# A list scheduler's priorities and assumed durations, changed in an attention and feed-forward layer

## The reference

```python
# step 1: causal attention on the normalised rows, 16 heads of 16 numbers
qkv = layernorm(x) @ w_qkv                       # then Q, K, V per head
Q, K = apply_rope(Q), apply_rope(K)              # rotate by position
attn = softmax(where(causal, Q @ K.T * 0.25, -1e6))
x = x + (attn @ V) @ w_proj + b_proj
# step 2: two products, and the length of the pair
y = layernorm(x)
x = x + sqrt((y @ cos(theta + theta_noise))**2 + (y @ sin(phi + phi_noise))**2)
```

## Time and profile before

| what | value |
|---|---|
| time, median of 3 executions (lowest to highest) | 1993.34 us (1989.42 to 1999.2) |
| the profiled execution: its own time, and its span | 1999.2 us, 1997.5 us |
| PE busy, share of the span | 1951.3 us, 98% |
| DVE | 1562.7 us, 78% |
| ACT | 1390.4 us, 70% |
| PEld (weight loads) | 796.1 us, 40% |
| POOL | 871.5 us, 44% |
| DMA, mean of 16 engines | 67 GB/s, 0.2 of their time |

### The profile page before, as it was taken

One profiled execution on the slowest core, in us unless ns is written; L12 is line 12 of the kernel. 1 busy time (PEld: TensorE's weight loads), 2 busy tenths in 40 slices (PEclk: granted clock), 3 DMA queues, 4 the chain that ended last, 5 costly groups with the idle time before them and its releaser, 6 DMA issues.

```text
span 1997.5 us, 38166 instructions
## 1 busy us (share of the span) xinstructions
PE 1951.3 (98%) x12020; PEld 796.1 (40%) x12020; DVE 1562.7 (78%) x4101; ACT 1390.4 (70%) x2687; POOL 871.5 (44%) x1336
## 2 busy tenths in 40 slices
PE   7999999999999999999999999999999999999998
PEld 4333432344434434344343343434443344333334
DVE  5898799977878788786887878788777758978735
ACT  3456777876676787766777777777767676777774
POOL 4714525445245463464445354453443545231222
PEclk9999999999999999999999999999999999999999
DMA  6301312122121221312222131222212131030131
GB/s 142 95 24 28 120 38 80 39 69 73 38 68 54 84 87 65 93 43 65 61 73 78 44 103 37 97 61 67 79 30 76 58 99 59 27 99 8 47 102 58
DMA packets 130762, 133.30 MB, mean 67 GB/s; under 512 B 29434, under 2 KB 105722, under 8 KB 130554
## 3 DMA queue, kind: packets, MB, share of 16 engines
q1 hardware_dynamic: 127728, 128.29, 21.0%
q10 hardware_dynamic: 2832, 2.56, 0.7%
HBM read 38.49 MB, written 25.68 MB: 32 GB/s over the span
## 4 chain that ended last, share of the span: by engine, by line
PE 85%; ACT 5%; issue 3%; DVE 2%; POOL 2%; DMA 2%; SPq 1%; DVEq 0%; ACTq 0%; POOLq 0%
PE banks L1059 22%; PE banks L1074 22%; PE banks L1037 22%; PE banks L981 6%; PE banks L992 5%; ACT probs L1178 3%; PE banks L926 3%; PE banks L1019 3%; DVE chunk_max L1379 1%; DMA squares<-sums 1%; SPq L739 1%; PE banks L915 1%; PE banks L908 1%; PE banks L1045 0%; ACT L1178 0%
## 5 line engine op out<-in xcount | busy, mean ns | idle before, releaser
L1178 ACT ACTIVATE probs<-banks 128x512 f32<-128x512 f32 (+1 forms) x2240 | 1144.5, 602 | 356.3 <-PE banks L1059 270.1
L1379 DVE TENSOR_REDUCE chunk_max<-banks 128x1 f32<-128x512 f32 x1536 | 987.3, 683 | 246.3 <-PE banks L1037 243.3
L1059 PE MATMUL banks<-stack_q,stack_k 99*128 99x512 bf16 (+3 forms) x2560 | 736.5, 350 | 12.1 <-ACT probs L1178 4.3
L1037 PE MATMUL banks<-stack_k,stack_q 96*128 96x512 bf16 (+3 forms) x2560 | 709.7, 349 | 11.0 <-DVE chunk_max L1379 4.5
L1374 DVE CUSTOM_DVE_ANT_0 banks<-banks,row_mask 128x128 f32<-128x128 f32 (+3 forms) x1024 | 483.9, 508 | 74.1 <-PE banks L1037 72.9
L1074 PE MATMUL banks<-probs,v_one 128*17 128x512 f32 (+3 forms) x5120 | 531.0, 533 | 2.0 <-POOL probs L1506 0.8
L1059 PEld LDWEIGHTS banks<-stack_q,stack_k 99*128 99x128 bf16 x2560 | 230.6, 97 | 430.3 <-ACT probs L1178 229.0
L1037 PEld LDWEIGHTS banks<-stack_k,stack_q 96*128 96x128 bf16 x2560 | 232.9, 97 | 328.9 <-DVE chunk_max L1379 80.9
L1506 POOL TENSOR_SCALAR_AFFINE_SELECT probs<-probs 128x512 f32<-128x512 f32 x256 | 161.9, 641 | 378.4 <-ACT probs L1178 378.0
L1074 PEld LDWEIGHTS banks<-probs,v_one 128*17 128x17 f32 x5120 | 118.0, 96 | 263.7 <-issue 177.8
L1374 DVE DVE_READ_ACCUMULATOR2_ANT chunk_max<- 128x1 f32 x1024 | 144.2, 141 | 0.0
(11 more groups left out here) (158 smaller groups left out, 1162.2 us busy)
## 6 DMA issues: line engine op xcount, KB each, us to landing
stack_q<-parts SPq DMA_DIRECT2D x384, 64.0 KB, 2.6
stack_k<-parts SPq DMA_DIRECT2D x354, 64.0 KB, 2.6
sums<-o_raw SPq DMA_DIRECT2D x64, 256.0 KB, 2.4
rot<-raw SPq DMA_DIRECT2D x236, 64.0 KB, 2.0
xin<-x SPq DMA_DIRECT2D x16, 512.0 KB, 3.9
mid<-x SPq DMA_DIRECT2D x13, 512.0 KB, 4.9
heads_t<-sums SPq DMA_DIRECT2D x26, 256.0 KB
inverse<-inverses SPq DMA_DIRECT2D x26, 256.0 KB
```

Source lines behind the costliest of these rows:

```text
L1037: mm = nc.tensor.matmul(bank[:, n * wide:(n + 1) * wide], stack_q[u % 2][0:SPLIT_ROWS, t, h + n, j * P:(j + 1) * P], stack_k[u % 2][0:SPLI ...
L1059: mm = nc.tensor.matmul(bank[:, a * wide:(a + 1) * wide], stack_k[u % 2][0:ROWS, j // SUB, first + a, (j % SUB) * P:(j % SUB + 1) * P], st ...
L1178: nc.scalar.activation(probs[:, g % PROBS, first:first + many, w0:SPAN], bank, ACT.Exp).then_inc(s_exp, 1)
L1379: nc.vector.tensor_reduce(to, bank[:, 0:count * wide].rearrange("p (h n) -> p h n", h=count), AX.X, ALU.max).then_inc(s_emptied["DVE"], 1)
```

## The change

Only numbers in `plan()` and its constants are changed; no instruction is added or taken away except fillers, and no tile, bank range or engine changes. The due times, the patience, the charge for a change of kind, and a set of assumed durations are other numbers, so the five lists come out in another order. The core of the diff (left out are more lines of the same two kinds, among them those for the loads of `x`, `rot`, `rows`, `heads`, `keepinv`, `inverse` and `store`, whose assumed durations fall as `fetch`'s does):

```diff
-URGENT = .526
+URGENT = 1.0
...
-MAX_LEAD = .578
-QK_LEAD = .737
+MAX_LEAD = 0.56
+QK_LEAD = 0.5
-EARLY = .545
-V_LEAD = .418
-SLACK = .9
-PATIENCE = .008
+EARLY = 0.75
+V_LEAD = 0.5
+SLACK = 0.4
+PATIENCE = 0.1
...
-TURN_COST = .1
-STICK = 0
-RUN = 4.358
+TURN_COST = 0.13
+STICK = 0.02
+RUN = 2.0
...
-                job(("fetch", u, c), "SP", 7.8, at, ...
+                job(("fetch", u, c), "SP", 5.4, at, ...
-                with_bank(name, name, "DVE", (0.17 if d == tile // SUB and masks(n) else 0.07 / n) * n + wide / 970, ...
+                with_bank(name, name, "DVE", (0.13 if d == tile // SUB and masks(n) else 0.07 / n) * n + wide / 970, ...
-            job(("bias", n), "POOL", 2.5, at, [("x3", n), ("bias", n - 1)])
+            job(("bias", n), "POOL", 1.3, at, [("x3", n), ("bias", n - 1)])
-                job(("dev3", n), "POOL", 3.2, at + 0.1, [("stats3", n), ("apply3", n - 1)])
+                job(("dev3", n), "POOL", 2.8, at + 0.1, [("stats3", n), ("apply3", n - 1)])
```

38 lines of the change are left out of this document (19 added, 19 removed).

## The result

The changed kernel takes 2022.0 us in the median of 4 executions (2016.0 to 2026.1), the kernel before 1994.4 in its 4: a ratio of 1.0139, 95% interval [1.0111, 1.0166]. The forecast was 2013 us with a range of 1996 to 2037, and 70% on slower. So the sign and the range are right and the size is 9 us short. The profiled execution of after took 2022.4 us, which is its median; that of before was 5.9 us above the median of three, 1993.3, that the forecast starts from. The two traces therefore show 23.1 us of difference in their spans (1997.5 to 2020.6), and I explain those.

The account below looks back on a forecast made before the run. PE, busy 98% of the span, was taken to set the time through nearly the whole run. 10.6 + 3 + 4 + 3.8 - 1.5 = +19.9 us on a median of 1993.3 gave 2013 us, range 1996 to 2037.

Parts of the forecast that it names:

- (a): PE's whole list: 101 more changes between column layouts at 0.105 us each, hidden by nothing; +10.6 us.
- (b1): Start: V's projection, now earlier, waits for its weights, first maxima 2.8 to 4.7 us late; +3 us (-1 to +8).
- (b2): Finish of a block: less PE work between proj and transposes, so waits in 12 blocks; +4 us (0 to 18).
- (b3): Score and maximum passes: more quick bank refills behind maxima, fewer behind scores; +3.8 us (-4.7 to +8.5).
- (b4): End of the run: 4 fillers instead of 11 after the last values; -1.5 us, or 0.
- At no cost: SP's shorter assumed times cost nothing; only unit 14's last pair of rows could cost up to 6 us once.
- No change: Rival: PE has slack that absorbs layout changes; about 1995 us, up to 2003; chance 0.20.
- Much slower: Rival: finish waits reaching 2 us in half of the 12 blocks bring the lower clock; 2036 us; chance 0.22.
- decides from waits of 2 us on: Lower-clock rival's threshold: PE waits of 2 us or more bring the lower clock; at 0.35 nothing happens.
- Faster: Rival: keeping closer to due times halves PE's 46.2 us without a matmul; 1979 us; chance 0.08.

Follow-up runs that it names:

- the fifty splits: Kernel before with 50 runs of values products split in two by a maximum product, 739 layout changes becoming 839; ratio 1.0047.
- a_invert: Changed kernel with block 11's reciprocal moved 14 places later in DVE's list; ratio 1.0129.
- b_ce: Kernel before with the changed kernel's rules of choice and engine times; due times and SP's assumed times stay before's; ratio 1.0078.
- a_choice: Changed kernel with the four rules of choice (PATIENCE, TURN_COST, STICK, RUN) set back to before's; ratio 1.0058.
- b_eng: Kernel before with only the assumed times of the engines set to the changed kernel's; ratio 1.0012.
- the square of runs: Due times of after or before, crossed with short or long SP times: after 1.0139 (short), 1.0164 (long); before 1.0372 (short), 1.0078 (long).
- a_due: Changed kernel with the due times and leads set back to before's, SP's assumed times still short; ratio 1.0372, 2068 us.
- a_sp: Changed kernel with only SP's nine assumed times set back to before's longer ones; ratio 1.0164.
- a_fill: Changed kernel with 20 instead of 4 filler products in front of the first V projection; ratio 1.0144.
- a_fix: Changed kernel with V's weights loaded before the first fetches, block 11's denominators loaded earlier and its reciprocal 6 places later; ratio 1.0113.
- a_fix2: a_fix plus block 11's input load and inverses load placed around unit 15's second fetch on SP, and DVE's scale 6 places later; ratio 1.0100.
- a_wv: Changed kernel with the load of V's weights moved in front of the first fetches in SP's list; ratio 1.0108.

## Why the prediction was right, and where it wasn't

**(a) right in kind and size.** Predicted +10.6 for 101 changes; the fifty splits give 0.104 each, so +10.5. It is the largest term, and the one that the direct experiment bears out.

**(b1) right in its mechanism, too small.** The wait for V's weights was foreseen, and they were there when computed (PE starts on them at 31.65, within 30.3 to 32.2). PE got to them at 28.2 and not at 25.5, so it waited 3.4 us and not 4.8 to 6.7. The start cost +7.3 (8.9 less unit 0's 1.6) where I took 3 and had 8 as the upper end. What was left out is the clock: the first maxima came at 36.90 and not at 33.0 to 34.9, and of the 5.25 us from V's projection to them 2.5 were clock; a second stretch at 0.50 follows from 53.9 to 64.1. About 1 us of the 7.3 is luck: `a_invert` has the same lists here but no low clock in the first block's projection, and its excess in front of the first scores is 1.0 less.

**(b2) about the right size (+6.6 for +4), by another mechanism.** I argued from the distance between `proj` and the transposes. But in the run `b_ce` all twelve finishes are short, 8.9 to 11.8 us, and have 6.5 us of excess together, as much as before's long ones (6.2). What differs is POOL's list. In after a rotation step starts between DVE's sum and the block's deviation (`L669`):

```profile
799.75 0.38 DVE L1272 BATCH_NORM_AGGREGATE mv<-stats 128x2 f32<-128x6 f32 x4
...
800.05 1.27 POOL L646 TENSOR_TENSOR turned<-raw,cos_t 128x512 f32<-128x512 f32 x1 [4.01 <-ACT raw L1138]
801.40 0.23 POOL L669 TENSOR_SCALAR variance<-mv 128x4 f32<-128x4 f32 x1
...
808.08 0.63 PE L915 MATMUL banks<-ident,inverse 128*128 128x128 f32 x4 [0.28 <-DVE chunk_max L1379]
```

In `b_ce` POOL is free there:

```profile
793.12 0.38 DVE L1272 BATCH_NORM_AGGREGATE mv<-stats 128x2 f32<-128x6 f32 x4
...
793.66 0.23 POOL L669 TENSOR_SCALAR variance<-mv 128x4 f32<-128x4 f32 x1 [0.29 <-DVE mv L1272]
```

From the end of the sum it is 1.27 us in the one and 0.16 in the other. The masks of the diagonal's last probabilities stand behind that on POOL, and values wait 0.2 to 0.3 us for them; the transposes wait 0.3 to 0.4 for their bank. The prediction had the rotation step (1.29) as an upper case; it was the rule: the same 1.27 to 1.28 us stand in nine of after's twelve finishes, and in none of `b_ce`'s. In `a_choice` they stand in nine too, with 1.36 to 1.39 us of excess each where `b_ce` has 0.38 to 0.64, and `b_eng`'s three finishes of 8.9 us, with POOL free, have 0.64 each. It is not the whole of it: two of after's finishes with POOL free have 1.0 and 1.6 us. That the mask and the bank carry the cost is read from waits, and no run took the rotation step away.

**(b3) wrong in sign, -4.2 for +3.8, near the lower bound (-4.7).** The counts were right (maxima more often, scores less), but the price was not a constant. Behind scores the excess in front of refills in under 0.7 us is 14.7 us in 74 before (0.20 each) and 4.3 in 59 after (0.07); behind maxima it is 2.4 in 6 (0.40) and 8.6 in 23 (0.37). So the maxima's term was about right (+6.2 for +8.5), and the scores' was twice too small (-10.4 for -4.7). Most of the drop is in unit 0: 37 such refills with 6.9 us before, 36 with 0.8 after. A distance in PE's list doesn't say when the reader gets there. The term also left out the unmasked maxima, for whose reader (`L1379`) the maxima wait 4.5 us in 16 before and 9.3 in 23 after, 4.0 of it in unit 14.

**(b4) right.** The end, from the last values on, went from 36.2 to 34.0 us; -1.5 predicted for the fillers. The rest of the 2.2 is in other rows of the end.

**"At no cost" is the step that failed.** For the shorter SP times I looked at what PE needs from transfers, and kept 6 us for a pair of rows behind a fetch in unit 14. The loss came in unit 14 (+8.6, with 6.8 us at the lower clock in it), but by an operation that PE doesn't read: DVE's reciprocal, which stood in DVE's list in front of ready maxima. I had not compared the place of DVE's and POOL's transfer-bound operations with SP's list. That this step can be dear is shown by the square of runs, not by after itself: 58 us between `a_due` and `b_ce`. With after's due times the longer times gained nothing (`a_sp`), so how much of after's own 28 us this step cost stays open.

The misses in the profiled pair: start +4.3, finishes +2.6, unit 14 +8.6, refills -8.0, the end, (a) and the rest -4.3; together +3.2, which is 23.1 less 19.9. So the size looks better than it is, and this part is luck: (b3)'s error offset unit 14's. The other 6 us between 2013 and 2022 come from the two profiled executions: before's was 5.9 us above the 1993.3 that I started from, after's at its median, so the medians are further apart (28.7 us, or 27.7 from before's 1994.4 of four) than the traces. These 6 us are in neither trace and stay unexplained, beyond that single stretches at the lower clock come and go (last section).

**The rivals.** "No change" is out by the fifty splits. "Much slower" was right in that waits bring the lower clock, and wrong in its point of decision (below). "Faster" is out; waits for exponentials and masked maxima did shrink by 2.6 us, as it said, but those for unmasked maxima and for masked probabilities grew by 4.8 and 4.1, and the layout changes came on top.

## What to carry to other kernels

In a program of in-order lists a planner's assumed duration isn't a free parameter: a transfer assumed shorter than it is can put its reader too early in some engine's list, and everything ready behind the reader waits too. Compare the place of each transfer-bound operation with the real time of the issues in front of its load, on every engine, before calling such a change free. When a wait is removed and the time stays, look for the same microseconds on the next list of the chain, and edit the list where they arise. Count layout changes in PE's list (0.1 us each here); they are the one term that nothing hid. And add up the time at the lower clock in both traces before pricing waits: here some 8 of the 15 us of excess fell into it.

## What the runs showed of the hardware

The lower clock can follow on short waits, and not every time. PE's waits in front of 841 us, in after and (the last of the same three) in the run `a_invert`, whose lists are the same up to there:

```profile
840.53 0.39 PE L1037 MATMUL banks<-stack_k,stack_q 96*128 96x512 bf16 x1 [0.57 <-DVE chunk_max L1379]
841.22 0.22 PE L1045 MATMUL banks<-ident_bf,max_parts 128*48 128x128 bf16 x1 [0.30 <-DVE chunk_max L1379]
841.89 0.34 PE L1059 MATMUL banks<-stack_q,stack_k 99*128 99x384 bf16 x1 [0.46 <-ACT probs L1178]
```

```profile
840.60 0.34 PE L1061 MATMUL banks<-stack_q,stack_k 99*128 99x384 bf16 x1 [0.46 <-ACT probs L1180]
```

And the stretch that follows, length, busy us of PE, PEld, DVE, ACT, POOL, granted clock, DMA share, GB/s, for after and for `a_invert`:

```profile
841.20:848.00 6.80, 5.98 (x39) 2.53 (x39) 6.59 (x27) 6.46 (x15) 5.14 (x8) 1.00 0.24 65
```

```profile
841.20:848.00 6.80, 6.80 (x30) 2.27 (x27) 4.85 (x22) 4.48 (x10) 5.02 (x9) 0.50 0.41 120
```

All three waits are the same to a hundredth in both, none over 0.6 us, and one execution runs on at 2.4 GHz (1.00) while the other is at 1.2 GHz (0.50) for the next 6.8 us and has 2.3 us more of excess in that unit. Four of the five profiled runs that keep after's list but for single entries show it (`a_fill`, `a_invert`, `a_fix`, `a_fix2`), `a_wv` and after itself don't. So the prediction's "decides from waits of 2 us on" does not hold: the clock fell in four executions behind three waits of 0.3 to 0.6 us close together, and stayed up behind the same three in two. What else decides it, these runs don't show.

A change of column layout cost 0.104 us, in the mean of the 100 that the fifty splits added.
